# A transformer-like kernel of four layers: values turned through DRAM, and the relative terms added where the scores lie

## The chip, the cores and the metric

The kernel runs as one program on one core of a Trainium2 chip. A core has TensorE (PE, matrix products from SBUF into PSUM), VectorE (DVE), ScalarE (ACT), GpSimd (POOL) and SyncE (SP, which here only issues DMAs), each with a queue of its own; they wait for each other by semaphores. The metric is the device time of one execution in microseconds.

## What is computed

Four layers, each `x = x + layer(_gn(x))` on `x` of shape (4, 16, 16, 1024). Layer 0 is a lambda layer, layer 3 a tensor-train convolution; the change touches layers 1 and 2, which are attention over 16 heads of 64 channels. Layer 1 has a mask, layer 2 has position terms:

```python
# layer 1, per head
s = jnp.where(mask, jnp.einsum('bhqe,bhke->bhqk', q, k) * scale, min)
o = jnp.einsum('bhqk,bhke->bhqe', softmax(s), v)
# layer 2
qkv = hidden_states @ qkv_w + qkv_b
attn = jnp.einsum('bqc,bkc->bqk', q * scale, k)
rel_h = jnp.einsum('bhwc,hkc->bhwk', rq, Rh)
rel_w = jnp.einsum('bhwc,wkc->bhwk', rq, Rw)
attn = attn + rel_h[:, :, :, :, None] + rel_w[:, :, :, None, :]
out = softmax(attn, axis=-1) @ v
return out @ proj_w + proj_b
```

`rel_h` and `rel_w` use the query without the scale; `Rh` and `Rw` are rows of small tables, picked by the distance of key and query.

## The kernel before

Layers 1 and 2 are worked through in four stages `s` (layer 1 and 2, each in two halves of two images) of eight items `j`; an item `i = 8 s + j` is a pair of heads on 512 tokens. There are 32 items, 0 to 31 (`LAST`), of which 16 to 31 are layer 2. Every product is made of three float32r products (hi x hi, lo x hi, hi x lo), so a projection Q, K or V of one item is 8 chunks x 3 = 24 matmuls of 128x512, and one O block (output projection, eight per stage) as many.

The order of TensorE is written out in `attention_pe`: in an ordinary item scores(i) (`scores`, four banks from `S` = 2), `relative(i + 1)`, K(i + 1), `attend(i - 1)` (probabilities times values), V(i), and Q(i + 2) with `turn_values(i)` after its second chunk. In an item with j = 0 the eight O blocks of the stage before stand ahead of Q. In the last stage the first four chunks of O blocks 0, 1 and 2 are put between the last items' work, and `build_m` (a matrix for layer 3) between the rest.

The other engines, each in its own written order (`attention_act`, `attention_dve`):
- ScalarE evicts the products' high parts (`evac_q`, `evac_k`, `evac_v`, `evac_o`), takes the exponentials (`exps(i, k)`, four per item, one bank of 2 x 256 scores each), multiplies by the reciprocal sums (`normalize`), and evicts `relative`'s result (`evac_relative`). It also issues the write of the strips to DRAM.
- VectorE makes the low parts (`rest_of_q`, `rest_of_k`, `rest_of_o`), `maxima(i, k)`, the reciprocals (`invert_sums`), turns the probabilities in blocks of 32x32 (`turn_probs`), copies the values (`take_v`), adds O to `xT` (`add_out`) and makes the statistics (`stats_of`, `aggregate`, `group_stats`).
- In items with j = 1 to 4 both also make the next stage's norm: `norm.y` and `norm.head` on ScalarE, `norm.y` and `norm.rest` on VectorE; `norm.coefficients` (VectorE) comes before, after `norm.power` on GpSimd.
- The position terms: `relative(i)` multiplies the queries by the tables; the result goes to DRAM (`strips_to_dram`), and `strips_from_dram` reads it back with an offset per query, so that each query has its row term and its column term (`own_rel`). `sum_relative` adds both to a 512-wide tile `both_rel`, and `maxima` in layer 2 is one `scalar_tensor_tensor` (scores x SCALE + both_rel, in place) and one `tensor_reduce`.
- SP loads the weights in blocks of 256 KB (`w_load(n)`, three slots; GpSimd splits them into high and low part in `w_split`), and between them, at fixed places of the list of loads, the strips and the probabilities, which are written to DRAM and read back transposed (`probs_to_dram`, `probs_from_dram`, at `PROBS_AT`).

The values are turned on TensorE:

```python
for tt in range(4):
    m = nc.tensor.transpose(PS[:, turned_bank(i), tt * P:tt * P + P], vT[:, tt * P:tt * P + P], ident[:, :])
m.then_inc(v_tr, 1)
```

## Time and profile before

| | us |
|---|---|
| median of 3 runs (lowest, highest) | 1244.37 (1243.34, 1245.15) |
| the profiled execution | 1246.36 |
| its span | 1244.4 |
| TensorE busy | 1216.4 (98%) |
| VectorE, ScalarE, GpSimd busy | 690.4, 475.1, 641.5 |

The span is the time from the first to the last instruction. A matmul's busy time overlaps that of the next, so the distance between groups, not the busy time of one, is what a group costs. In the order of time, layer 0 takes 0 to 251 us, layer 1's two stages up to 706, layer 2's up to 1130 and layer 3 the rest.

### The profile page before, as it was taken

The numbers are of one execution on the slowest core, as the hardware profiler recorded it, in microseconds if no ns is written. First come the engines' busy times: TensorE is split into PE (matmuls) and PEld (weight loads), VectorE is DVE, ScalarE is ACT, GpSimd is POOL, SyncE is SP. The second block draws the span as 40 slices with busy tenths as digits, with TensorE's granted clock in tenths as the row PEclk, the third lists the DMA queues.
The fourth block names the chain that finished last, engine by engine and source line by source line (L and its number), as shares of the span: only waits on it lengthen the run. The fifth ranks groups of instructions, "written<-read, shape, count | busy, mean of one in ns | idle before, by whom it ended". The sixth has DMA issues, their size and how long they took to land.

```text
span 1244.4 us, 19555 instructions
## 1 busy us (share of the span) xinstructions
PE 1216.4 (98%) x6768; PEld 975.0 (78%) x6768; DVE 690.4 (55%) x1434; ACT 475.1 (38%) x1229; POOL 641.5 (52%) x726
## 2 busy tenths in 40 slices
PE   6999999999999999999999999999999999889998
PEld 4788896478888888888888878777887787668887
DVE  7534444775665433666452578756347776476212
ACT  3611141034645320656341164644206555243212
POOL 4633389256565567555546655555665556464000
PEclk9999999999999999999999999999999999999999
DMA  5211124025564643454645356557535565620012
GB/s 185 84 46 48 34 56 117 8 65 160 154 169 137 184 134 97 127 177 128 185 136 166 86 160 212 180 160 223 168 102 151 175 209 156 205 60 1 29 40 68
DMA packets 129376, 155.03 MB, mean 125 GB/s; under 512 B 30080, under 2 KB 84000, under 8 KB 129280
## 3 DMA queue, kind: packets, MB, share of 16 engines
q1 hardware_dynamic: 118976, 146.92, 39.7%
q10 hardware_dynamic: 10304, 6.88, 1.8%
q8 instruction: 54, 0.88, 0.3%
q14 instruction: 42, 0.34, 0.1%
HBM read 111.81 MB, written 37.75 MB: 120 GB/s over the span
## 4 chain that ended last, share of the span: by engine, by line
PE 89%; DVE 5%; ACT 2%; issue 1%; DMA 1%; SPq 1%; POOL 0%; ACTq 0%; DVEq 0%; POOLq 0%
PE PS L1137 53%; PE PS L682 7%; PE PS L1758 7%; PE PS L1183 4%; PE PS L960 3%; PE PS L969 2%; PE PS L975 2%; PE PS L1227 2%; PE PS L1216 2%; PE PS L1775 2%; PE PS L1247 2%; PE PS L665 1%; PE PS L1197 1%; DVE bst L257 1%; PE PS L700 1%
## 5 line engine op out<-in xcount | busy, mean ns | idle before, releaser
L1137 PE MATMUL PS<-XB,w_hi 128*128 128x512 f32 x1024 | 340.5, 397 | 1.2 <-POOL w_lo L228 1.2
L226 POOL CAST w_hi<-w_raw 128x512 fp32r<-128x512 f32 x195 | 124.2, 637 | 307.5 <-PE PS L1137 213.0
L228 POOL TENSOR_TENSOR w_lo<-w_raw,w_hi 128x512 fp32r<-128x512 f32 x195 | 256.1, 1313 | 15.6
L1137 PEld LDWEIGHTS PS<-XB,w_hi 128*128 128x128 f32 x1024 | 192.2, 188 | 47.1 <-issue 5.0
L1137 PE MATMUL PS<-XB,w_lo 128*128 128x512 f32 x512 | 200.2, 391 | 0.0
L1137 PE MATMUL PS<-XB,part 128*128 128x512 f32 x768 | 190.3, 394 | 0.0
L1137 PEld LDWEIGHTS PS<-XB,part 128*128 128x128 f32 x768 | 141.9, 188 | 32.2 <-issue 2.3
L1373 ACT ACTIVATE part<-PS,nmax 128x256 f32<-128x256 f32 (+1 forms) x256 | 112.2, 443 | 141.6 <-DVE nmax L1485 93.2
L1383 ACT ACTIVATE part<-part,prec 128x256 f32<-128x256 f32 (+1 forms) x256 | 105.8, 476 | 27.7 <-DVE prec L1500 27.7
L228 POOL TENSOR_TENSOR part<-part,part 128x512 fp32r<-128x512 f32 x85 | 111.5, 1312 | 6.8
L1137 PE MATMUL PS<-part,w_hi 128*128 128x512 f32 x344 | 112.9, 395 | 1.5 <-DVE part L1544 1.5
L226 POOL CAST part<-part 128x512 fp32r<-128x512 f32 x85 | 54.1, 636 | 116.3 <-PE PS L1137 103.7
L1137 PEld LDWEIGHTS PS<-XB,w_lo 128*128 128x128 f32 x512 | 96.2, 188 | 18.5 <-issue 0.2
L1496 DVE STREAM_TRANSPOSE part<-part 128x384 f32<-128x384 f32 (+1 forms) x128 | 82.1, 641 | 49.9 <-ACT part L1383 49.9
L1137 PEld LDWEIGHTS PS<-part,w_hi 128*128 128x128 f32 x344 | 65.2, 190 | 15.9 <-ACT part L1427 1.9
L682 PE MATMUL PS<-XB,w_hi 128*128 128x512 f32 x256 | 70.9, 392 | 0.0
L1137 PE MATMUL PS<-part,w_lo 128*128 128x512 f32 x172 | 67.6, 393 | 0.0
L1397 ACT ACTIVATE part<-PS,bias 128x512 fp32r<-128x512 f32 x16 | 11.0, 688 | 143.1 <-PE PS L1137 143.1
L1506 DVE COPY part<-PS 128x512 f32<-128x512 f32 x32 | 22.1, 692 | 78.2 <-PE PS L1197 78.2
L1137 PE MATMUL PS<-part,part 128*128 128x512 f32 x252 | 62.9, 399 | 0.2 <-issue 0.2
L1539 DVE TENSOR_TENSOR part<-part 128x512 f32<-128x512 f32 x64 | 59.4, 947 | 0.0
L598 DVE COPY part<-PS 64x512 f32<-64x512 f32 x32 | 34.6, 1080 | 44.2 <-PE PS L700 43.9
(136 smaller groups left out, 1884.0 us busy)
## 6 DMA issues: line engine op xcount, KB each, us to landing
w_raw<-in_w SPq DMA_DIRECT2D x187, 256.0 KB, 2.8
part<-in_w SPq DMA_DIRECT2D x85, 256.0 KB, 2.8
turned<-part SPq DMA_DIRECT2D x128, 128.0 KB, 2.9
part<-turned SPq DMA_DIRECT2D x32, 512.0 KB, 5.0
turned<-part SPq DMA_DIRECT2D x128, 96.0 KB, 2.5
part<-turned SPq DMA_DIRECT2D x32, 384.0 KB, 4.0
strips<-part ACTq DMA_DIRECT2D x16, 256.0 KB, 2.7
out_x<-xT SPq DMA_DIRECT2D x16, 256.0 KB, 2.1
```

Of the source, the lines that this page charges most:

```text
L226: pool.tensor_copy(hi, raw).then_inc(w_hi_done, 1)
L228: pool.tensor_tensor(lo, raw, hi.bitcast(F32), ALU.subtract).then_inc(w_ready, 1)
L598: last = nc.vector.tensor_copy(dst, src)
L682: m = nc.tensor.matmul(PS[:, 2 * (n % 2) + h, :], wt[:, (c % 4) * P:(c % 4) * P + P], x_part(hl, h, c), start=c == k == 0, stop=c == CK - ...
L960: m = nc.tensor.matmul(bank[0:rows * SIDE, (x - x0) * w:(x - x0) * w + w], table, Qs[:, jp, x * N + SIDE * y0:x * N + SIDE * y1], start=jp ...
L1137: m = nc.tensor.matmul(PS[:, bank, :], wt[:, (c % 4) * P:(c % 4) * P + P], rhs(hl, c), start=c == k == 0, stop=c == CK - 1 and k == 2)
L1183: m = nc.tensor.matmul(PS[:, S + 2 * a + hh, at + lo:at + hi], x[rows, qs], y[rows, cols], start=k == 0, stop=k == 2)
L1373: last = nc.scalar.activation(prob[:, n % 2, at:at + hi - lo], PS[:, S + k, qt * N + lo:qt * N + hi], ACT.Exp, bias=nmax[:, k, qt:qt + 1], ...
L1383: last = nc.scalar.activation(p, p, ACT.Copy, scale=prec[:, k, qt:qt + 1])
L1496: nc.vector.transpose(dst, src).then_inc(t_done, 1)
L1539: nc.vector.tensor_tensor(both_rel[:, n % 2, :, :, :], of_row, of_col, ALU.add).then_inc(rel_sum, 1)
L1758: m = nc.tensor.matmul(PS[:, bank, :], x3(hl, b, c, tt * P), w[:, c, half * HALF:half * HALF + HALF], start=c == k == 0, stop=c == CK - 1 ...
```

## The change

1. Values. `turn_values` moves from TensorE to VectorE: V's bank is turned in blocks of 32x32 into `vB`, written to DRAM in four pieces and read back (`values_to_dram`, `values_from_dram`), and `take_v`, now on ScalarE, copies it to `v`. `evac_v` is gone; V's bias is added to the attention's output in `evac_o` and `rest_of_o`.
2. `relative` has the tables as stationary and 512 queries as moving operand, three matmuls; its bank is turned by VectorE (`turn_relative`), and ScalarE issues four writes of strips, in runs of 32 elements, after the second `exps`.
3. `sum_relative` and `both_rel` are gone. `maxima` adds the row terms to the bank with one `tensor_tensor`, and then, for each half, adds the column terms, multiplies by -SCALE and takes the minimum in one `tensor_tensor_reduce`. The tables are divided by SCALE on GpSimd, and `exps` has a scale of -1 in layer 2.
4. Order. `attend(i - 1)` stands behind V(i) and Q(i + 2); with j = 0 Q(i + 2) stands ahead of the O blocks. `evac_o(i - 2)` and `rest_of_o(i - 2)` come in the middle of an item. Each item's probabilities go out in four writes instead of eight, a block of weights later. At the end the first halves of six O blocks, not three, stand between the last items.

TensorE in layer 2, from the last scores of item 25 to its K product, before (part_79 to part_82 are the queries, part_90 and part_91 the tables):

```order
L1183 MATMUL PS<-part_77,part_81 128x256 x2
L1247 MATMUL PS<-part_90,part_80 128x64 [waits v_evac_151,tables_ready_182,q_lo_155,q_hi_154]
L1247 MATMUL PS<-part_90,part_80 128x64
L1247 MATMUL PS<-part_91,part_80 128x64 x2
L1247 MATMUL PS<-part_90,part_82 128x64 x2
L1247 MATMUL PS<-part_90,part_80 128x64 x2
```

The same place now (part_88 and part_89 are the tables):

```order
L1177 MATMUL PS<-part_77,part_81 128x256 x2
L1225 MATMUL PS<-part_80,part_88 128x512 [waits tables_ready_180,q_lo_154,q_hi_153]
L1225 MATMUL PS<-part_80,part_89 128x512
L1225 MATMUL PS<-part_82,part_88 128x512
L1135 MATMUL PS<-XB,part_54 128x512 [waits w_ready_40,k_lo_156,k_hi_155]
```

Twelve rows with 24 matmuls have become three matmuls; the wait for `q_lo` has stayed in front of them.

ScalarE in a layer 2 item, from the second `exps` to the third, before (part_86 holds the probabilities, part_92 `all_rel`):

```order
L1373 ACTIVATE part_86,psum<-PS,nmax 128x256
L1383 ACTIVATE part_86<-part_86,prec 128x256 [waits p_rec_162,p_exp_161]
L1383 ACTIVATE part_86<-part_86,prec 128x256
L1383 ACTIVATE part_86<-part_86,prec 128x256 [waits p_rec_162,p_exp_161]
L1383 ACTIVATE part_86<-part_86,prec 128x256
L1407 ACTIVATE part_92<-PS 128x8x32 [waits rel_done_173,strips_out_175]
L1407 ACTIVATE part_92<-PS 128x8x32 [waits rel_done_173]
L1626 DMA strips<-part_92 128x4x128 [waits rel_evac_174]
L1373 ACTIVATE part_86,psum<-PS,nmax 128x256 [waits t_done_164,p_max_160]
```

And now (part_85 the probabilities, part_90 `all_rel`, part_83 `v`, part_84 `vB`, part_75 the attention's output):

```order
L1344 ACTIVATE part_85,psum<-PS,nmax 128x256
L1611 DMA strips<-part_90 512x1x32 [waits rel_evac_173]
L1611 DMA strips<-part_90 512x1x32 x3
L1354 ACTIVATE part_85<-part_85,prec 128x256 [waits p_rec_161,p_exp_160]
L1354 ACTIVATE part_85<-part_85,prec 128x256
L1354 ACTIVATE part_85<-part_85,prec 128x256 [waits p_rec_161,p_exp_160]
L1354 ACTIVATE part_85<-part_85,prec 128x256
L1333 ACTIVATE part_83<-part_84 128x512 [waits o_done_168,v_in_151]
L1390 ACTIVATE part_75<-PS,bias 128x512 [waits o_done_168]
L1344 ACTIVATE part_85,psum<-PS,nmax 128x256 [waits t_done_163,p_max_159]
```

The write of the strips stands ahead of both `normalize`, four issues instead of one; the values' copy and O's eviction have come before the third `exps`.

VectorE after the last O block of a stage, before:

```order
L337 TENSOR_SCALAR gn<-gn 128x1 [waits hn_step_63]
L342 COPY gn_wide<-gn 128x32 [waits hn_rstd_64]
L343 SCALAR_TENSOR_TENSOR gn_wide<-gn 128x32
L393 STREAM_TRANSPOSE coef<-gn_wide 128x64 [waits hn_wide_65]
L1515 SCALAR_TENSOR_TENSOR part_81<-PS,bias,part_79 128x512 [waits q_hi_154]
L1539 TENSOR_TENSOR part_83<-part_93 128x512 [waits rel_added_179,strips_in0_176] x2
L1482 SCALAR_TENSOR_TENSOR PS<-PS,part_83 128x512 [waits rel_sum_178,s_done_158]
L1485 TENSOR_REDUCE nmax<-PS 128x2 [waits rel_added_179]
```

And now (ISA is the `tensor_tensor_reduce`, and after each the read of its accumulator):

```order
L337 TENSOR_SCALAR gn<-gn 128x1 [waits hn_step_63]
L1457 TENSOR_TENSOR PS<-PS,part_91 128x512 [waits strips_in0_175,s_done_157]
L1462 ISA PS,nmax<-PS,part_91 128x256 [waits rel_added_177]
L1462 ISA nmax 128x1
L1462 ISA PS,nmax<-PS,part_91 128x256
L1462 ISA nmax 128x1
L1516 STREAM_TRANSPOSE part_90<-PS 128x512 [waits strips_out_174,rel_done_172]
```

The next item's first `maxima` follows the group statistics directly; the queries' low part has moved ahead of the O blocks' additions, and the coefficients to the end of the item.

The diff, without the semaphores' declarations and repeated details:

```diff
             take_block(i, "V", range(0 if i else 1, 2))
+            if i + 2 < ITEMS:
+                take_block(i + 2, "Q")
...
+    values = nc.dram_tensor("values", (2, P, 4 * P), F32).ap()
+    turned = nc.dram_tensor("turned", (2, P, 8 * N), F32).ap()
...
+            for k, (x, y) in enumerate(((rel_hi, qh[i % 2]), (rel_lo, qh[i % 2]), (rel_hi, ql[i % 2]))):
+                m = nc.tensor.matmul(PS[:, X, :], x.rearrange("p r n -> p (r n)"), y.rearrange("p (a y x) -> p y a x", a=2, y=SIDE),
+                                     start=k == 0, stop=k == 2)
+            m.then_inc(rel_done, 1)
...
         for i in range(1, LAST - 1):
             score_block(i)
             project(i + 1, "K", range(CK))
-            attend(i - 1, 0)
-            attend(i - 1, 1)
             project(i, "V", range(CK))
-            if i % PAIRS == 0:
-                s = i // PAIRS - 1
-                out_block(s, 0, range(CK))
-                out_block(s, 1, range(0, 2))
-                turn_values(i)
-                out_block(s, 1, range(2, CK))
-                for o in range(2, CK):
-                    out_block(s, o, range(CK))
+            if i % PAIRS:
                 project(i + 2, "Q", range(CK))
+                attend(i - 1, 0)
+                attend(i - 1, 1)
             else:
-                project(i + 2, "Q", range(0, 2))
-                turn_values(i)
-                project(i + 2, "Q", range(2, CK))
+                attend(i - 1, 0)
+                attend(i - 1, 1)
+                project(i + 2, "Q", range(CK))
+                for o in range(CK):
+                    out_block(i // PAIRS - 1, o, range(CK))
         i = LAST - 1
         score_block(i)
         project(LAST, "K", range(CK))
+        project(i, "V", range(CK))
         attend(i - 1, 0)
         attend(i - 1, 1)
-        project(i, "V", range(CK))
         scores(LAST, 0)
         scores(LAST, 1)
-        out_block(3, 0, range(0, 2))
-        turn_values(i)
-        out_block(3, 0, range(2, 4))
+        out_block(3, 0, range(0, 4))
         project(LAST, "V", range(CK))
+        for o in (1, 2):
+            out_block(3, o, range(0, 4))
         attend(i, 0)
         attend(i, 1)
-        out_block(3, 1, range(0, 4))
-        turn_values(LAST)
-        out_block(3, 2, range(0, 4))
-        for o in range(3):
-            out_block(3, o, range(4, 7))
+        for o in (3, 4, 5):
+            out_block(3, o, range(0, 4))
         attend(LAST, 0)
         attend(LAST, 1)
-        for o in range(3):
-            out_block(3, o, range(7, CK))
+        for o in range(6):
+            out_block(3, o, range(4, CK))
             for k in M_AFTER[o, 1]:
                 build_m(k)
-        for o in range(3, CK):
+        for o in range(6, CK):
             for half in range(2):
                 out_block(3, o, range(4 * half, 4 * half + 4))
                 for k in M_AFTER[o, half]:
                     build_m(k)
...
+        def take_v(i):
+            act.wait_ge(v_in, 16 * (i + 1))
...
+                act.wait_ge(o_done, 2 * i)
+            dst = v.rearrange("p t (b c) -> p t b c", b=4)
+            nc.scalar.activation(dst, vB.rearrange("p (b t c) -> p t b c", b=4, t=4), ACT.Copy).then_inc(v_ready, 1)
...
             j, s = i % PAIRS, i // PAIRS
-            if i:
+            if i and (i < PAIRS or j != 1):
                 evac_q(i + 1)
             exps(i, 0)
             exps(i, 1)
+            if LO_KEYS <= i + 1 < ITEMS:
+                strips_to_dram(act, i + 1)
             normalize(i, 0)
             normalize(i, 1)
-            evac_relative(i + 1)
+            if 0 < i < LAST:
+                take_v(i - 1)
+            if i >= 2 and j != 1:
+                evac_o(i - 2)
             exps(i, 2)
             normalize(i, 2)
+            if i == LAST:
+                take_v(i - 1)
             exps(i, 3)
-            if i and j == 0:
-                evac_o(i - 1)
             normalize(i, 3)
             evac_k(i + 1)
-            if j:
-                evac_o(i - 1)
-            evac_v(i)
             if 1 <= j <= 4:
                 for c in (2 * j - 2, 2 * j - 1):
                     norm.y(nc.scalar, s + 1, c)
                 for c in (2 * j - 2, 2 * j - 1):
                     norm.head(s + 1, c)
+            if i == LAST or i and j == 0:
+                evac_o(i - 1)
+            if i and j == 0:
+                evac_q(i + 2)
+        take_v(LAST)
...
-                dve.wait_ge(rel_sum, n - 4 * LO_KEYS + 1)
-                nc.vector.scalar_tensor_tensor(scores, scores, SCALE, both_rel[:, n % 2, :, :, :].rearrange("p a h w -> p (a h w)"),
-                                               ALU.mult, ALU.add).then_inc(rel_added, 1)
+                a, hh = k // 2, k % 2
+                dve.wait_ge(strips_in[a], 16 * 4 * (i - LO_KEYS + 1))
+                of_row, of_col = (own_rel[:, r, 2 * a:2 * a + 2, 32 * hh:32 * hh + SIDE] for r in range(2))
+                whole = scores.rearrange("p (a h w) -> p a h w", a=2, h=SIDE)
+                of_row = of_row.rearrange("p a (h w) -> p a h w", w=1).broadcast_to([P, 2, SIDE, SIDE])
+                nc.vector.tensor_tensor(whole, whole, of_row, ALU.add).then_inc(rel_added, 1)
                 dve.wait_ge(rel_added, n - 4 * LO_KEYS + 1)
-                last = nc.vector.tensor_reduce(nmax[:, k, :], scores.rearrange("p (a n) -> p a n", a=2), AX, ALU.max, negate=True)
+                for qt in range(2):
+                    tile = whole[:, qt, :, :]
+                    of_key = of_col[:, qt, :].rearrange("p (h w) -> p h w", h=1).broadcast_to([P, SIDE, SIDE])
+                    last = nc.vector.tensor_tensor_reduce(tile, tile, of_key, -SCALE, 3.0e38, ALU.add, ALU.min,
+                                                          accum_out=nmax[:, k, qt:qt + 1])
...
+        def turn_values(i):
+            product_done(dve, (i, "V"))
             if i:
-                dve.wait_ge(o_done, 2 * i)
-            nc.vector.tensor_copy(v.rearrange("p a n -> p (a n)"), PS[:, turned_bank(i), :]).then_inc(v_ready, 1)
+                dve.wait_ge(v_ready, i)
+            src = PS[:, bank_of(i, "V"), :].rearrange("p (t q c) -> p t q c", t=4, q=4)
+            dst = vB.rearrange("p (q t c) -> p t q c", q=4, t=4)
+            nc.vector.transpose(dst, src).then_inc(v_turned, 1)
...
+        def turn_relative(i):
+            if i == ITEMS or layer_of(i) == 1:
                 return
-            n, a, hh = 4 * i + k, k // 2, k % 2
-            dve.wait_ge(strips_in[a], 16 * 4 * (i - LO_KEYS + 1))
-            of_row, of_col = (own_rel[:, r, 2 * a:2 * a + 2, 32 * hh:32 * hh + SIDE] for r in range(2))
-            of_row = of_row.rearrange("p a (h w) -> p a h w", w=1).broadcast_to([P, 2, SIDE, SIDE])
-            of_col = of_col.rearrange("p a (h w) -> p a h w", h=1).broadcast_to([P, 2, SIDE, SIDE])
-            if n >= 4 * LO_KEYS + 2:
-                dve.wait_ge(rel_added, n - 4 * LO_KEYS - 1)
-            nc.vector.tensor_tensor(both_rel[:, n % 2, :, :, :], of_row, of_col, ALU.add).then_inc(rel_sum, 1)
+            dve.wait_ge(rel_done, i - LO_KEYS + 1)
+            if i > LO_KEYS:
+                dve.wait_ge(strips_out, 64 * (i - LO_KEYS))
+            nc.vector.transpose(all_rel, PS[:, X, :]).then_inc(rel_evac, 1)
...
-            if i:
+            if i and (i < PAIRS or j != 1):
                 rest_of_q(i + 1)
-            sum_relative(i, 0)
-            sum_relative(i, 1)
             maxima(i, 0)
+            turn_relative(i + 1)
             maxima(i, 1)
             invert_sums(i, 0)
-            sum_relative(i, 2)
             invert_sums(i, 1)
+            maxima(i, 2)
             turn_probs(i, 0)
-            maxima(i, 2)
             turn_probs(i, 1)
-            sum_relative(i, 3)
+            if i >= 2 and j != 1:
+                rest_of_o(i - 2)
+            maxima(i, 3)
             invert_sums(i, 2)
-            maxima(i, 3)
             turn_probs(i, 2)
-            if i and j == 0:
-                rest_of_o(i - 1)
+            if i == LAST:
+                turn_values(i)
             invert_sums(i, 3)
             turn_probs(i, 3)
             if i < LAST:
                 rest_of_k(i + 1)
-            if j:
+            if i < LAST:
+                turn_values(i)
+            if i and j == 0:
                 rest_of_o(i - 1)
-            if i and j == 0:
-                take_v(i)
-            if i and j == 0:
+                rest_of_q(i + 2)
                 for o in range(CK):
                     add_out(s - 1, o)
                     if o:
                 stats_of(s - 1, CK - 1)
                 norm.aggregate(s + 1, range(CK), 16)
                 norm.group_stats(s + 1)
-            if j or i == 0:
-                take_v(i)
-            if j == 0:
+            if j == 1:
                 norm.coefficients(s + 1)
...
+        sp.wait_ge(rel_evac, done + 1)
+        rows = strips[buf].rearrange("(ax y) n -> ax y n", y=SIDE)
+        for b in range(4):
+            src = all_rel[32 * b:32 * b + 32, :].rearrange("p (y n) -> p y n", y=SIDE)
+            sp.dma_start(rows[:, :, 32 * b:32 * b + 32], src).then_inc(strips_out, 16)
...
-    def probs_to_dram(sp, i, a):
+    def probs_to_dram(sp, i, a=None):
         run = 2 * squares(i) * 32
-        sp.wait_ge(t_done, 4 * i + 2 * a + 2)
+        sp.wait_ge(t_done, 4 * i + (2 if a == 0 else 4))
...
+            row = probB[32 * q:32 * q + 32, 0:8 * run].rearrange("p (b r) -> p b r", b=4)
+            at, w = (0, 2 * run) if a is None else (a * run, run)
+            to = bass.AP(turned.tensor, (i % 2) * P * 8 * N + 2 * q * run + at, [[8 * N, 32], [32 * 8 * N, 4], [1, w]])
+            sp.dma_start(to, row[:, :, at:at + w]).then_inc(p_out[a or 0], 16)
...
+    def values_to_dram(sp, i):
+        sp.wait_ge(v_turned, i + 1)
...
+        for b in range(4):
+            to = bass.AP(values.tensor, (i % 2) * P * 4 * P + P * b, [[4 * P, 32], [32 * 4 * P, 4], [1, P]])
+            sp.dma_start(to, vB[32 * b:32 * b + 32, :].rearrange("p (q r) -> p q r", q=4)).then_inc(v_out, 16)
+    def values_from_dram(sp, i):
+        sp.wait_ge(v_out, 64 * (i + 1))
+        sp.dma_start(vB, values[i % 2, :, :]).then_inc(v_in, 16)
...
+    STRIPS_AT = [slots[(i + 1, "K"), 1] if i < LAST else slots[(i, "V"), 0] for i in range(ITEMS)]
+    PROBS_AT = [slots[(i + 1, "V"), 1] for i in range(LAST - 1)] + [slots[(3, "O", 1), 0], slots[(3, "O", 5), 0]]
...
+                if n == PROBS_AT[i] and i < LAST:
+                    probs_to_dram(sp, i)
+                    values_to_dram(sp, i)
+                if n == PROBS_AT[i] + 1 and i < LAST:
                     probs_from_dram(sp, i, 0)
-                if n == PROBS_AT[i] + 2:
                     probs_from_dram(sp, i, 1)
+                if n == PROBS_AT[i] + 2 and i < LAST:
+                    values_from_dram(sp, i)
```

## Rows read from the trace of the kernel before

**Rows 1.** The page's part 1: busy us, share of the span, instructions of each engine.
```profile
PE 1216.4 (98%) x6768; PEld 975.0 (78%) x6768; DVE 690.4 (55%) x1434; ACT 475.1 (38%) x1229; POOL 641.5 (52%) x726
```

**Rows 2.** The chain in order of time, item 26: start us, us, what.
```profile
950.97 1.62 PE PS L1183 x24
952.59 1.51 PE PS L1247 x24
954.10 5.66 PE PS L1137 x24
959.77 1.88 PE PS L1216 x16
...
968.67 0.44 PE PS L1197 x4
...
973.24 1.62 PE PS L1183 x24
```

**Rows 3.** ScalarE's timeline in layer 1: start, us, instruction, idle before it.
```profile
344.00 0.60 ACT L1361 ACTIVATE part<-PS 128x512 f32<-128x512 f32 x1 [2.32 <-PE PS L1137]
```

**Rows 4.** TensorE's timeline: scores of item 30, layer 3's first product.
```profile
1040.01 1.69 PE L1183 MATMUL PS<-part,part 64*128 64x256 f32 x24
...
1129.94 8.34 PE L1758 MATMUL PS<-part,XB 128*128 128x512 f32 x36
```

**Rows 5.** TensorE's waits: us in total, times, longest us.
```profile
PE PS L1216 <- DMA part<-turned: 2.3, 4, 1.1
```

**Rows 6.** Issue of DMAs: SP's writes and reads of probabilities, ScalarE's queue in layer 0.
```profile
L1649 SPq DMA_DIRECT2D turned<-part x256: 303/442/1461, 284.9 to 1077.9; - x128
...
DMA to landing us min/median/max: 3.3/4.4/6.9
...
197.64 3.84 ACTq L900 DMA_DIRECT2D part<-part  x6
```

**Rows 7.** VectorE's timeline in item 18 (j = 2).
```profile
731.27 0.69 DVE L1482 SCALAR_TENSOR_TENSOR PS<-PS,part 128x512 f32<-128x512 f32 x1
...
732.60 0.69 DVE L1482 SCALAR_TENSOR_TENSOR PS<-PS,part 128x512 f32<-128x512 f32 x1
...
743.35 0.71 DVE L1496 STREAM_TRANSPOSE part<-part 128x512 f32<-128x512 f32 x1 [1.03 <-ACT part L1383]
...
746.87 0.73 DVE L408 TENSOR_SCALAR part<-xT,coef 128x256 f32<-128x256 f32 x2
748.04 2.56 DVE L419 TENSOR_TENSOR XB<-part,XB 128x512 fp32r<-128x512 f32 x2 [0.45 <-ACT XB L414]
```

**Rows 8.** ScalarE's timeline in the same item.
```profile
734.05 0.48 ACT L1373 ACTIVATE part<-PS,nmax 128x256 f32<-128x256 f32 x1 [0.31 <-DVE nmax L1485]
...
734.96 1.70 ACT L1383 ACTIVATE part<-part,prec 128x256 f32<-128x256 f32 x4
...
737.24 0.37 ACTq L1626 DMA_DIRECT2D strips<-part  x1
737.97 0.47 ACT L1373 ACTIVATE part<-PS,nmax 128x256 f32<-128x256 f32 x1 [0.76 <-DVE nmax L1485]
...
739.70 0.91 ACT L1383 ACTIVATE part<-part,prec 128x256 f32<-128x256 f32 x2 [0.72 <-DVE prec L1500]
741.10 0.47 ACT L1373 ACTIVATE part<-PS,nmax 128x256 f32<-128x256 f32 x1 [0.49 <-DVE nmax L1485]
```

**Rows 9.** VectorE's groups by line: busy us, mean ns, idle before.
```profile
L1539 DVE TENSOR_TENSOR part<-part 128x512 f32<-128x512 f32 x64 | 59.4, 947 | 0.0
...
L1475 DVE TENSOR_TENSOR PS<-PS,maskb 128x256 f32<-128x256 f32 x64 | 26.6, 415 | 1.2 <-PE PS L1183 1.2
```

**Rows 10.** VectorE's timeline after the last O block of stage 2.
```profile
923.28 0.75 DVE L1553 SCALAR_TENSOR_TENSOR xT<-PS,bias,xT 128x512 f32<-128x512 f32 x1 [4.03 <-PE PS L1137]
...
927.64 0.15 DVE L337 TENSOR_SCALAR gn<-gn 128x1 f32<-128x1 f32 x1
```

**Rows 11.** Busy us in one stretch of the tail, then granted clock, DMA share, GB/s.
```profile
1098.40:1101.40 3.00, 3.00 (x8) 2.32 (x7) 1.84 (x2) 0.19 (x1) 2.69 (x3) 0.50 0.02 8
```

208 lines of the change are left out of this document (88 added, 120 removed).

## The prediction

> **What bounds the kernel now.** I read four views. First the busy time: TensorE works in 1216.4 us of a span of 1244.4 us [rows 1], so almost all of the time is its own queue of matmuls, and an edit pays by what it takes out of that queue and costs by what it makes the queue wait for. Second the chain that ended last, in order of time. It shows one item of layer 2 with no gap: scores 1.62, `relative` 1.51, K, `attend` 1.88, V, the four transposes 0.44, Q, and the next scores 22.27 us after the last [rows 2]. Third, since TensorE is full, how near the others are to becoming the bound. In layer 1 ScalarE stands idle for 2.32 us before V's eviction [rows 3], with nothing queued behind it that TensorE needs. In layer 2, items with j = 1 to 4 also carry the norm of the next stage, and there VectorE and ScalarE have a chain of nearly the period's length (below). Fourth the end: from the scores of item 30 to layer 3's product the kernel takes 1129.94 - 1040.01 = 89.9 us, with several waits in it [rows 4].
>
> I call the start of the first `maxima` of an item m, counted from the start of the item's scores; it needs half of the 1.62 us of scores, so m is 0.85 where VectorE is free. A norm item is one with j = 1 to 4.
>
> **What leaves TensorE.** (a) `turn_values` goes: 32 times 0.44 us [rows 2] = 14.1 us. (b) `relative` becomes 3 matmuls of 512 columns instead of 24 of 64. The product's matmuls of the same width take 5.66 us for 24 [rows 2], so at most 0.24 each; without the change of tile shape they follow at 0.227, 24 in 5.46, or 0.68 for three. 1.51 - 0.68 = 0.83, 16 times = 13.3 us. The bounds are 0.68 and the 1.51 of before. (c) `attend` waited for its probabilities for 2.3 us in all [rows 5], at most 1.1 at a time; it now stands behind V and Q, 11 us later, which covers the way through DRAM. I count 0.7 us of it here and the rest in the tail.
> The period of a layer 2 item becomes 22.27 - 0.44 - 0.83 = 21.0 us.
>
> **The tail (d)**, by the new order, 0 at the scores of item 30: scores 1.62, relative 0.68, K 5.7, V 5.5, attend 1.9 end at 15.4. `scores(31)` then wait for `k_lo` until 18.3 (worked out below) and end at 20.0. Half an O block (2.75), V (5.5), two halves (5.5), attend (1.9) and three halves (8.2) end at 43.8. The second half of the last `attend` waits, in my count, until 45.5: the queue of SP has eight writes before it, 0.44 us each, and the read lands 4.4 us after its issue [rows 6]. The other 120 matmuls take 27.3, sixteen `build_m` 3.9, a wait on them 1.0, changes of shape 0.6. End at 79.4 instead of 89.9: 10.5 less, of which (a) and (b) hold 1.7. I take 8.5 us for the waits alone; between 4 and 10.
> Sum of what leaves: 14.1 + 13.3 + 0.7 + 8.5 = 36.6 us.
>
> **What the loop of VectorE and ScalarE costs.** In layer 2 the next `relative` needs `q_lo`, which VectorE makes after the norm's work. Before, from m (731.27) to the end of the norm's last subtraction (748.04 + 2.56 = 750.60) are 19.33 us [rows 7]. I change the path piece by piece:
> - From m to the second `exps`: 734.05 - 731.27 = 2.78 [rows 7, 8]. Now two maxima with `turn_relative` between them. A transpose of 512 columns is 0.71 [rows 7]. A maximum was two scans, 732.60 - 731.27 = 1.33 [rows 7]. Now it is one scan of 512 (0.69 and 0.04 for its semaphore) and two of 256, each with a read of its accumulator. The instruction isn't in the trace. A sum of 256 columns on a bank took 0.415 [rows 9], and I give the small read 0.1: 0.73 + 2 x 0.51 = 1.75. Bounds: 1.33, if the two are one scan; 2.3, if everything goes at the rate of the sum of two SBUF tiles, 0.947 for 512 [rows 9], with 0.2 per read. 2 x 1.75 + 0.70 + 0.05 = 4.25: +1.47.
> - Before the first `normalize` ScalarE now issues four writes of the strips. One took 0.37 [rows 8]; six others on this queue took 3.84, 0.64 each [rows 6]. I take 0.5: +2.0 (1.5 to 2.6). Behind them on ScalarE stand both `normalize`, and behind these VectorE's transposes.
> - From the end of both `normalize` (734.96 + 1.70) to the third `exps` 1.31 [rows 8], before for `evac_relative` and a wait; now `take_v` and `evac_o`, 0.65 each (a copy of 512 columns is 0.60 [rows 3]): 0.
> - Third `exps` to its `normalize` 1.73 [rows 8]; now `rest_of_o` 0.7, `maxima` 1.75 and the reciprocal with the hand-overs 0.3 stand before it, 2.75: +1.0. To the fourth `exps` 1.40 [rows 8], now 0.85, since its maximum is already there: -0.55.
> - From the last transpose of probabilities to the norm's `y` 3.52 (743.35 to 746.87 [rows 7]), which held `rest_of_o`, `take_v` and a wait for TensorE; now `rest_of_k` and `turn_values`, 1.95 in all: -1.57.
> - `rest_of_q` 0.7 closes the loop; the two sums of tables that followed it are gone.
> 19.33 + 1.47 + 2.0 + 1.0 - 0.55 - 1.57 + 0.7 = 22.4 us, against a period of 21.0. So each norm item is paced by this loop and TensorE waits 1.4 us at the next `relative`. `k_lo` comes at m + 17.4, early enough in the others, so items without a norm keep 21.0; in layer 1 no `relative` waits, and the loop is shorter.
> The first norm item (j = 1) costs more. Before, the Q product (5.5 us) lay between the last O block and the next scores, and covered VectorE's last sum, statistics and aggregate: 923.28 to 927.64 + 0.15, that is 4.5 us, about 4.6 from O's end [rows 10]. Now Q stands ahead of the O blocks, the cover is gone, and m = 4.6 instead of 0.85. The loop there is 22.3 (without `evac_o` and `rest_of_o` 1.35 less; `coefficients`, three small instructions like the one of 0.15 [rows 10] with their semaphores, 0.6 more, and ScalarE's `y` behind them 0.65). `q_lo` comes at 26.9, `relative` could start at 21.0 + 1.6 = 22.6: a wait of 4.3 us.
> A stage of layer 2 loses 4.3 + 3 x 1.4 = 8.5, two lose 17.0 us. With the low bounds of both prices the loop is 20.6 and 5 us are lost; with the high ones 24.6, and 34.6 us.
>
> **What I cost at nothing.** `turn_values` on VectorE in layer 1 and `take_v` on ScalarE take the place of `take_v` and `evac_v` there. The five DMAs of the values per item lie behind the probabilities' four (eight before) on SP; SP blocks on `v_turned` until about m + 18, but the next weights are needed some 6 us after that at the earliest. If that cover were gone TensorE would wait at a product for what SP is late.
>
> **A rule of the skill.** The strips were written in runs of 512 B and now in runs of 128 B (2048 a matrix). The landing of the write isn't critical in the trace: strips are issued by m + 7.2 and must be in DRAM by about m + 17. The Trainium skill, "DMA: Bandwidth & Descriptors", Specifications, says that below 512 B the DMA engine does read-modify-write, which speaks against this write; no run yet shows it here. A second, "Vector Engine (DVE) Microarchitecture Reference", section 7, says that the kind of instruction with an accumulator halves its rate with two SBUF sources that aren't bf16; here one is a PSUM bank, so by that page the 2.3 above wouldn't come and the maximum stays near 1.75.
>
> **The rivals.**
> 1. The loop fits: maximum 1.33, issues 0.37. Only the 2.5 us after each O stage stay: 36.6 - 5.0 = 31.6 off, 1212.8 us. For it: VectorE's pieces overlap in the trace. Against: four scans with reads where two stood.
> 2. Slower: the maximum with accumulator is slow. With x us above 1.75 the loop grows by 3x, a stage by 12x, both by 24x. The gain of 19.6 is gone at x = 0.8, a maximum of 2.55 us, or 0.9 us for each of the 256-column instructions with its read. At 3.0 it is 1244.4 - 19.6 + 30 = 1255. Nothing on a bank in the trace is so slow for its size.
> 3. The strips come late: if the small writes land after 11 us (2.7 before), the eight norm items wait 1 us more each: 1233.
> 4. It doesn't do what it says in part: `relative` reads its moving operand in runs of 16 and takes 1.5 us as before: 13.3 less, 1238.
> A fall of the clock could add to any: in the tail, after several waits, the granted clock was 0.50 for 3 us [rows 11] (the 1.2 GHz level), in which 8 matmuls ran instead of 13, 1.2 us lost. The waits of 4.3 us could bring two such stretches.
>
> **How the numbers follow.** The profiled execution has a span of 1244.4 and took 1246.36, 2.0 above the median of the runs; the gain is taken off the median. 36.6 - 17.0 = 19.6: 1244.4 - 19.6 = 1224.8, so 1225. Chances: this forecast 0.63, rival 1 0.14, rival 2 0.11, rival 3 0.06, rival 4 0.06. The range reaches from rival 1 with a slightly better tail, 1211, to 1241, which holds rivals 3 and 4 and most of the high bounds. A measurement of this kernel can tell about 0.2% from no change. Faster by more: the forecast, 1, 3 and 4 less their edges, 0.86; within 0.2% 0.04; slower 0.10.
>
> **What would show it.** Right: 0.44 us transposes and 64-column matmuls gone from the chain; items without a norm 21.0 us apart, in layer 1 20.0; waits of about 4 us at `relative` of items 18 and 26, about 1.4 in the three after each; `scores(31)` waiting about 3 us for `k_lo`. Wrong: the 256-column instruction far from 0.4 us, the ACT queue's issues far from 0.5, no wait at items 18 and 26, or waits at `attend` or at the products' weights.

## The result, and the profile after

The changed kernel takes **1264.57 us** (1262.71 to 1265.41, 4 runs) against 1244.22 us (1243.34 to 1245.15, 4 runs) for the kernel before on the same chip: a ratio of 1.016, 95% interval 1.0144 to 1.0179. The prediction was 1225 us, faster. It is slower by 20.3 us, 40 us off the forecast. The profiled execution has a span of 1263.0 us. The ratios, here and below, use the fast executions of each kernel alone.

In the kernel after, some names have other lines: `scores` L1177, `relative` L1225, `attend` L1198 (layer 2) and L1209 (layer 1); `take_v` on ScalarE L1333; `evac_o` L1390 and `rest_of_o` L1525; the maximum's two instructions L1457 (row term) and L1462 (column term, scale, maximum); `rest_of_k` L1505; on ScalarE's queue the strips' writes L1611; on SP's queue the probabilities' writes L1635 and reads L1646, the values' writes L1655 and read L1659, the strips' reads L1623.

The page's part 1 of after, for [rows 1]:
```profile
PE 1194.4 (95%) x6304; PEld 960.8 (76%) x6304; DVE 645.6 (51%) x1578; ACT 458.2 (36%) x1197; POOL 630.2 (50%) x727
```
TensorE is busy for 22 us less. The count was 27 us less; e5 below has the same matmuls, and they are busy for another 10 us less (1184.2), at a granted clock of 0.996 instead of 0.985. But it no longer works for nearly the whole span: 69 us of it are idle, against 28 before.

**Where the time went.** I took the starts of `scores` of all items from TensorE's timeline, which gives the period of each item. In layer 1 they are 19.7 us apart (before 20.4) as long as all is well, items 1 to 7 and 9 to 10. From item 11 on some take 20.2 to 21.9. In layer 2 they are 22.0, 27.1, 25.1, 23.0, 25.0, 21.8, 25.5 (items 17 to 23) and 21.5, 26.3, 24.1, 24.3, 24.8, 23.5 (25 to 30), where before nearly each took 22.3 (item 30: 17.0). Busy time in these two stretches, after first, then before (columns: from and to, us, busy time of PE, PEld, DVE, ACT, POOL, granted clock, DMA share, GB/s):
```profile
700.90:870.40 169.50, 153.65 (x808) 121.18 (x807) 100.97 (x275) 76.35 (x211) 80.21 (x85) 0.94 0.68 192
938.80:1083.30 144.50, 121.45 (x667) 96.34 (x667) 86.81 (x242) 65.80 (x182) 67.65 (x70) 0.98 0.67 188
```
```profile
705.70:862.80 157.10, 156.41 (x981) 124.01 (x980) 113.94 (x187) 81.81 (x226) 83.93 (x85) 1.00 0.58 174
928.60:1057.00 128.40, 127.87 (x815) 101.57 (x814) 96.89 (x162) 71.18 (x196) 71.54 (x70) 1.00 0.57 171
```
So the two stretches are 12.4 and 16.1 us longer. TensorE was busy for 2.8 and 6.4 us less in them, but stood idle for 15.9 and 23.1 us, and the granted clock, 1.00 before, was 0.94 and 0.98. Item 24, between them, takes 68.5 us instead of 65.8. Layer 1 (item 8 begins 6.3 us earlier, item 17 still 4.9) and the end (from `scores(31)` to layer 3's product 65.1 us instead of 73.0) give some of it back.

**What it waited for.** TensorE's waits of after, for [rows 5] (us in total, times, longest us):
```profile
PE PS L1225 <- issue: 17.0, 7, 2.9
PE PS L1177 <- DVE part L1505: 15.2, 11, 4.2
...
PE PS L1198 <- DVE part L1525: 6.1, 2, 3.8
```
`scores` wait for `k_lo`, `relative` for `q_lo` and `attend` for the `rest_of_o` of the item before. (The row of `relative` names no releaser; in item 18 `rest_of_q` ends at 727.33 and `relative` starts at 727.43.) All three come from VectorE, which is busy for only half of the time: it waits itself. ScalarE's waits show for what:
```profile
ACT part L1344 <- DVE nmax L1462: 161.1, 32, 49.4
ACT part L1333 <- DMA part<-values: 132.5, 31, 7.9
```
The second row is the one that matters. ScalarE stands for 132.5 us in front of `take_v`, in 31 of 32 items, since the values aren't back from DRAM. Item 22 shows how this reaches the others. ScalarE's timeline (start, us, instruction, idle before it):
```profile
829.23 1.39 ACTq L1611 DMA_DIRECT2D strips<-part  x2
830.73 1.71 ACT L1354 ACTIVATE part<-part,prec 128x256 f32<-128x256 f32 x4 [1.76 <-issue]
836.60 0.63 ACT L1333 ACTIVATE part<-part 128x512 f32<-128x512 f32 x1 [4.16 <-DMA part<-values]
837.14 0.67 ACT L1390 ACTIVATE part<-PS,bias 128x512 fp32r<-128x512 f32 x1
```
and the chain that ended last in the same stretch (start, us, what):
```profile
829.55 0.61 SPq L212
...
830.21 6.37 DMA part<-values
...
836.60 0.02 ACT part L1333
...
837.14 0.68 ACT part L1390
...
838.51 0.70 DVE PS L1457
...
843.91 0.72 DVE part L1505
...
844.88 1.70 PE PS L1177 x24
846.57 0.92 PE PS L1225 x3
847.49 2.75 PE PS L1135 x12
...
853.85 0.57 SPq L1646
...
855.13 6.95 DMA part<-values
```
This is a loop. The values' read of item 21 is issued at 830.21 and lands 6.37 us later. Behind it on ScalarE stand `take_v(21)`, `evac_o(20)` and the third `exps` of item 22, and so the second half of that item's softmax. Behind that on VectorE stands `rest_of_k(23)`, and `scores(23)` wait for it. Only when their product has used up weights can SP load new ones, and behind a load stand the probabilities' reads and the next values' read, 855.13. One turn takes 855.13 - 830.21 = 24.9 us; with TensorE never waiting it would be 21, by the prediction's count. The prediction called this place free.

Why does the read take so long? DMA issues of after, for [rows 6] (KB each, median us to landing):
```profile
values<-part SPq DMA_DIRECT2D x128, 64.0 KB, 2.5
part<-values SPq DMA_DIRECT2D x32, 256.0 KB, 5.9
```
A write of values lands after 2.5 us, the read of 256 KB after 5.9. On SP the read stands right behind two reads of probabilities (512 KB each in layer 2, 384 KB in layer 1) and a weight's load of 256 KB, so much of it may be time in a queue; e2 below tests that.

### The profile page after: what moved, and what is told of

Its sections match the earlier page's. It is cut to its first block, busy times and chain, and to the rows that moved or that the text cites. A ratio compares the mean times of both kernels' runs of the same rounds, so it can differ in the third digit from the quotient of the medians.

```text
span 1263.0 us, 18684 instructions
## 1 busy us (share of the span) xinstructions
PE 1194.4 (95%) x6304; PEld 960.8 (76%) x6304; DVE 645.6 (51%) x1578; ACT 458.2 (36%) x1197; POOL 630.2 (50%) x727
## 4 chain that ended last, share of the span: by engine, by line
PE 48%; DMA 13%; SPq 12%; DVE 10%; issue 7%; ACT 6%; POOL 3%; ACTq 1%; POOLq 0%; DVEq 0%
PE PS L1135 20%; DMA part<-values 11%; PE PS L1774 7%; PE PS L682 7%; SPq L1655 4%; SPq L1635 4%; PE PS L960 3%; SPq L212 2%; PE PS L969 2%; PE PS L975 2%; ACT part L1354 2%; DMA strips<-part 2%; PE PS L1791 2%; ACT part L1344 2%; SPq L1646 1%
## 5 line engine op out<-in xcount | busy, mean ns | idle before, releaser
L1135 PE MATMUL PS<-XB,w_hi 128*128 128x512 f32 x1024 | 335.4, 396 | 4.1 <-POOL w_lo L228 4.1
L226 POOL CAST w_hi<-w_raw 128x512 fp32r<-128x512 f32 x195 | 120.8, 619 | 327.1 <-PE PS L1135 172.7
L228 POOL TENSOR_TENSOR w_lo<-w_raw,w_hi 128x512 fp32r<-128x512 f32 x195 | 251.9, 1292 | 15.6
L1135 PEld LDWEIGHTS PS<-XB,w_hi 128*128 128x128 f32 x1024 | 194.9, 190 | 49.6 <-POOL w_lo L228 4.0
L1135 PE MATMUL PS<-XB,part 128*128 128x512 f32 x768 | 187.7, 393 | 0.0
L1135 PEld LDWEIGHTS PS<-XB,part 128*128 128x128 f32 x768 | 146.3, 191 | 31.2
L1135 PEld LDWEIGHTS PS<-XB,w_lo 128*128 128x128 f32 x512 | 97.4, 190 | 20.2 <-issue 0.2
L1135 PEld LDWEIGHTS PS<-part,w_hi 128*128 128x128 f32 x344 | 65.2, 190 | 15.5 <-issue 2.1
L1177 PE MATMUL PS<-part,part 64*128 64x256 f32 (+1 forms) x768 | 55.4, 292 | 19.4 <-DVE part L1505 15.2
L682 PE MATMUL PS<-XB,w_hi 128*128 128x512 f32 x256 | 70.9, 392 | 0.0
L1177 PEld LDWEIGHTS PS<-part,part 64*128 64x128 f32 x768 | 49.6, 194 | 27.8 <-issue 19.9
L1333 ACT ACTIVATE part<-part 128x512 f32<-128x512 f32 x32 | 20.2, 632 | 132.5 <-DMA part<-values 132.5
```

The lines of the kernel that those rows point to most:

```text
L226: pool.tensor_copy(hi, raw).then_inc(w_hi_done, 1)
L228: pool.tensor_tensor(lo, raw, hi.bitcast(F32), ALU.subtract).then_inc(w_ready, 1)
L682: m = nc.tensor.matmul(PS[:, 2 * (n % 2) + h, :], wt[:, (c % 4) * P:(c % 4) * P + P], x_part(hl, h, c), start=c == k == 0, stop=c == CK - ...
L1135: m = nc.tensor.matmul(PS[:, bank, :], wt[:, (c % 4) * P:(c % 4) * P + P], rhs(hl, c), start=c == k == 0, stop=c == CK - 1 and k == 2)
L1177: m = nc.tensor.matmul(PS[:, S + 2 * a + hh, at + lo:at + hi], x[rows, qs], y[rows, cols], start=k == 0, stop=k == 2)
```

## The experiments

**Theories.** T: the loop above, through `take_v`. R: the strips, written in runs of 128 B by four instructions instead of one in runs of 512 B, cost issue time on ScalarE and land late (median 5.8 us). M: the new maximum is slow. Each kernel was timed beside the one before on its chip. Items are numbered as above, and their lengths come from the starts of `scores` in the profiled execution.

### Take_v moved behind evac_k

```diff
-            if 0 < i < LAST:
-                take_v(i - 1)
             if i >= 2 and j != 1:
                 evac_o(i - 2)
...
             evac_k(i + 1)
+            if 0 < i < LAST:
+                take_v(i - 1)
```


> The changed kernel with one thing moved: ScalarE copies the values (take_v) behind evac_k instead of ahead of evac_o and the third exps. Theory T (the values' way through DRAM sets the pace: ScalarE stood 132.5 us before the 31 copies, with half of an item's softmax behind it): layer 2's items, 24 to 27 us apart now, come back to 21 to 23, and the kernel takes about 1245 us, 15 to 22 less than 1264.6. Rival R (the strips' small writes, landing after 5.8 us instead of 2.7, hold SP and all behind it): at most 4 us less. Rival M (the maximum's new form makes VectorE's loop too long): at most 4 us less.

Measured: 1230.66 us (1229.50 to 1231.78), ratio to before 0.989 [0.9873, 0.9902]. This is 34 us under the changed kernel, for an edit that removes no work and no DMA, and about twice what T expected: item 16 begins 8 us earlier than in the changed kernel, a gain in layer 1 that the expectation didn't count. `take_v`'s idle time, 132.5 us in the changed kernel, is here (us, times):
```profile
  DMA part<-values: 6.0, 4
```
The read still lands after 5.8 us, but nothing is behind it now. Items in layer 1 are 19.7 us apart throughout, in layer 2 mostly 20.2 to 22.4 (items 20, 26 and 28 take 26.2, 23.7 and 23.1).

### The values' read ahead of the probabilities' reads

```diff
                 if n == PROBS_AT[i] + 1 and i < LAST:
-                    probs_from_dram(sp, i, 0)
-                    probs_from_dram(sp, i, 1)
+                    values_from_dram(sp, i)
                 if n == PROBS_AT[i] + 2 and i < LAST:
-                    values_from_dram(sp, i)
+                    probs_from_dram(sp, i, 0)
+                    probs_from_dram(sp, i, 1)
```


> The changed kernel with the read of the values issued ahead of the two reads of the probabilities (1 MB) instead of behind them. T with the read's queueing as its cause: the values' read lands in about 3 us instead of 5.9 and starts about 1 us earlier, so each layer 2 item is up to 3 us shorter: about 1250 us. If the read's 5.9 us are not due to what is queued ahead of it: no change. Rivals R and M: no change.

Measured: 1228.03 us (1225.62 to 1233.87), ratio 0.988 [0.9844, 0.9908]. The second way to open the same loop gives the same, again more than the expectation had (1250 us). Issues, and `take_v`'s idle time:
```profile
part<-values SPq DMA_DIRECT2D x32, 256.0 KB, 3.1
```
```profile
  DMA part<-values: 35.4, 20
```
The read of the same 256 KB lands after 3.1 us in place of 5.9: 2.8 us were the queue. What is left on TensorE is the wait that the prediction spoke of, `relative` for `q_lo`:
```profile
PE PS L1225 <- issue: 13.3, 6, 3.2
```
It stands in items 18, 19, 21, 26, 27 and 29, which take 22.7 to 26.6 us, while nearly all others of layer 2 take 20.8.

### One write of the strips

```diff
-        for b in range(4):
-            src = all_rel[32 * b:32 * b + 32, :].rearrange("p (y n) -> p y n", y=SIDE)
-            sp.dma_start(rows[:, :, 32 * b:32 * b + 32], src).then_inc(strips_out, 16)
+        whole = strips[buf].rearrange("(t p) n -> p t n", p=P)
+        sp.dma_start(whole, all_rel.rearrange("p (t n) -> p t n", t=4)).then_inc(strips_out, 16)
```


> The changed kernel with the strips written by one DMA in runs of 512 bytes instead of four in runs of 128; the position terms are then those of wrong places, the work is otherwise the same. R: the whole loss of layer 2 goes, about 1240 us. T: ScalarE issues 1 DMA instead of 4 (some 2.3 us less an item) and SP gets its strips earlier, but the values still come last: 3 to 8 us less, about 1259. M: no change.

Measured: 1257.24 us (1253.87 to 1264.21), ratio 1.011 [1.0072, 1.0144]. This kernel leaves out the right places of the strips, so it computes wrong position terms with the same work. R is worth about 7 us here, the four executions reach from 0 to 11, and it doesn't explain the loss: ScalarE still waits for values, 167.9 us in all, and the loop stays closed.

### The kernel before, with the new maximum alone

Here `sum_relative` is gone and `maxima` is that of the change, with the tables scaled to fit it; the rest stays as it was.

> The kernel before with only the new form of the maximum (no sum_relative, tables divided by the scale on GpSimd, exps with a scale of -1). M: layer 2's items grow, 5 us or more slower than before. T and R: TensorE hides it, within 2 us of before; two sums of tables per item go and each maximum gets 0.2 us longer.

Measured: 1240.08 us (1239.72 to 1242.23), ratio 0.997 [0.9957, 0.9983]. M falls: this part alone is a gain of about 4 us (2 to 5 by the interval). In the trace of the changed kernel one whole maximum is (VectorE's timeline)
```profile
829.08 0.70 DVE L1457 TENSOR_TENSOR PS<-PS,part 128x512 f32<-128x512 f32 x1
829.81 0.43 DVE L1462 CUSTOM_DVE_ANT_1 PS<-PS,part 128x256 f32<-128x256 f32 x1
830.16 0.47 DVE L1462 CUSTOM_DVE_ANT_1 PS<-PS,part 128x256 f32<-128x256 f32 x1
```
829.08 to 830.63: 1.55 us, where I took 1.75, with bounds of 1.33 and 2.3. The first accumulator's read, 830.16 to 830.30, runs beside the second L1462.

### Both edits together

> The changed kernel with both earlier edits: take_v(i-1) behind evac_k(i+1) on ScalarE, and the values' read issued ahead of the probabilities' reads. Theory T (the take_v of one item, which waits for a read queued behind others, holds up the ScalarE work of the next item, in a loop): each edit alone opens that loop, so the two together give little over the better one: about 1225 us (1220 to 1228), items without a norm 20.8 us apart, the values' read landing after about 3 us. Theory L (what is left after that is the loop of VectorE and ScalarE in the norm items and at the stage boundary, as in the prediction): waits at relative in the norm items stay, 13 us or more in all. Rival Q (SP's queue is the second limit: values' and probabilities' transfers fill it whatever the order): 1230 or above, and waits at attend appear.

Measured: 1223.52 us (1221.45 to 1227.45), ratio 0.983 [0.9809, 0.9842]. With both ends of the loop open the changed kernel is 41 us faster and stands at the predicted time. ScalarE waits once more for values (7.1 us, the last item). What TensorE still waits for:
```profile
PE PS L1198 <- DMA part<-turned: 5.9, 5, 3.2
PE PS L1198 <- issue: 5.0, 4, 3.0
PE PS L1135 <- POOL w_lo L228: 3.8, 7, 1.2
PE PS L1209 <- issue: 3.8, 1, 3.8
PE PS L1225 <- issue: 3.0, 2, 1.5
```
The first and the third row are what SP brings, probabilities and weights. But most of the two rows of `attend` with no named releaser is `take_v`, now late on ScalarE. The 3.0 us are `attend(29)`; ScalarE's row and TensorE's:
```profile
1043.40 0.61 ACT L1333 ACTIVATE part<-part 128x512 f32<-128x512 f32 x1
1044.11 1.95 PE L1198 MATMUL PS<-part,part 128*64 128x256 f32 x16 [3.05 <-issue]
```
In item 16 it is the same: `take_v` ends at 643.71 and `attend(15)` starts at 643.81, after 3.79 us. So the late place has a price too.

### The Q product back behind the O blocks

The order of the stage boundary is as before the change, on TensorE and in the evacuations; all else as in the last kernel.

> e5 with the project(i + 2, 'Q') of a stage boundary back behind the O blocks, as it stood before. Theory L: the Q product covers VectorE's last sum, statistics and aggregate again; the prediction put 4.3 us of wait at relative of items 18 and 26 to this move, so the time falls by 5 to 9 us against e5 (of which 2 to 4 in the first norm item's scores). Rival S: the long first norm item is not from this cover, but from the strips' issues on ScalarE, so the time stays within 2 us of e5.

Measured: 1225.79 us (1223.24 to 1230.62), ratio 0.985 [0.9828, 0.9880]: no gain; L's 5 to 9 us didn't come. Items 18 and 26 now take 21.2 and 20.8 us instead of 22.5 and 22.5, and the ones after them 21.2 or less, so the cover that L speaks of is back. But items 8, 16 and 24, which hold the O blocks, take 65.7, 71.5 and 71.0 us against 63.5, 69.4 and 69.4: 2 us more each. TensorE's timeline shows a wait in each of them, 2.23, 2.22 and 1.61 us, at the O blocks, which now stand right behind `attend`; the releaser of the last is the `evac_o` on ScalarE. The gain at one end of the move is lost at the other.

### The strips issued behind normalize

```diff
-            if LO_KEYS <= i + 1 < ITEMS:
-                strips_to_dram(act, i + 1)
             normalize(i, 0)
             normalize(i, 1)
+            if LO_KEYS <= i + 1 < ITEMS:
+                strips_to_dram(act, i + 1)
```


> e5 with the four strips writes issued on ScalarE behind normalize(i, 1) instead of ahead of normalize(i, 0). Theory S (their issues, 0.56 to 2.0 us each by the profile of the change, delay normalize and so the VectorE work behind it): 2 to 3 us less in each of the six to eight norm items, 8 to 15 us off e5. Theory L without S (the loop is set by VectorE's own work): within 2 us of e5. Rival W (the strips' landing is late already): slower than e5, with waits of VectorE for strips at the next item's maxima.

Measured: 1223.33 us (1218.84 to 1227.77), ratio 0.983 [0.9802, 0.9857]. No difference from e5; the 8 to 15 us that S expected didn't come.

### One write of the strips, with the loop open

> e5 with the strips written by one DMA in runs of 512 B (in places that make wrong relative terms; the reads are as in the change). Theory S: like e7 or better, 8 to 15 us off e5, since three of four issues are gone and the write lands after about 2.7 us. Theory L without S: within 2 us of e5. If e8 gains and e7 does not, it is the landing and not the issue that costs.

Measured: 1213.04 us (1211.96 to 1214.76), ratio 0.975 [0.9733, 0.9763], 10.5 us under e5, in a kernel that leaves out the right places of the strips as e3 does. Its one write lands after 4.9 us (median), not after the 2.7 expected, and each of e5's four after 3.6. Ten of the twelve items 17 to 23 and 25 to 29 are now 20.8 us apart, all but two: item 18 with 25.3 and item 26 with 24.3. Item 18 on TensorE's timeline:
```profile
713.66 1.69 PE L1177 MATMUL PS<-part,part 64*128 64x256 f32 x24
718.24 0.96 PE L1225 MATMUL PS<-part,part 128*128 128x512 f32 x3 [2.90 <-issue]
```
and the windows of item 18 and of the one after it:
```profile
713.70:739.00 25.30, 22.41 (x119) 17.69 (x117) 19.69 (x41) 13.97 (x36) 13.66 (x14) 0.93 0.77 222
739.00:759.70 20.70, 20.70 (x117) 16.50 (x115) 15.65 (x37) 11.97 (x32) 11.35 (x13) 1.00 0.77 229
```
This is the wait at the boundary, in the item that the prediction named: 2.90 us idle, and a granted clock of 0.93 over the item, 0.50 (the 1.2 GHz level) from 719.2 to 722.0. Together it is about 4.5 us longer than its neighbour. In item 26 it is 1.90 us idle and 3.5 us in all.

### Take_v early at the boundaries, late elsewhere

```diff
-            if 0 < i < LAST:
+            if 0 < i < LAST and j == 0:
                 take_v(i - 1)
...
             evac_k(i + 1)
+            if 0 < i < LAST and j:
+                take_v(i - 1)
```
with the values' read first, as in e5.

> e5, but take_v(i-1) stands behind evac_k(i+1) only where j > 0; at a stage boundary (items 8, 16 and 24) it stands ahead of evac_o as in the change. Theory B: in e5 the late take_v costs at items 16 and 24, where attend(i-1) stands ahead of the O blocks and waits for it (69.4 us from item 16 and from item 24 to the next one, against 64.3 and 64.5 in e2): 5.1 + 4.9 = 10 us less than e5, so 1213 to 1215. Rival: those stages are long in e5 from the strips' issues or the DMA queue, so the time stays within 2 us of e5.

Measured: 1215.66 us (1212.81 to 1221.67, 5 runs), ratio 0.977 [0.9751, 0.9796]. 8 us under e5, and with the strips in their right places: **the best version, 29 us faster than the kernel before** (e13 below is level with it). The profiled execution is the slowest of the five, 1221.67 us. Item 16 takes 64.2 us (69.4 in e5), as expected. Item 24 didn't follow (69.6): there `attend(23)` waited 2.58 and 0.74 us for the probabilities' reads, which in this order stand behind the values'.

### The same narrow runs by one instruction

```diff
-        for b in range(4):
-            src = all_rel[32 * b:32 * b + 32, :].rearrange("p (y n) -> p y n", y=SIDE)
-            sp.dma_start(rows[:, :, 32 * b:32 * b + 32], src).then_inc(strips_out, 16)
+        to = bass.AP(strips.tensor, buf * HALF * P, [[32, 4], [SIDE * P, 32], [P, SIDE], [1, 32]])
+        sp.dma_start(to, all_rel.rearrange("p (y n) -> p y n", y=SIDE)).then_inc(strips_out, 16)
```


> e9 with the four strips writes of an item made by one instruction, to the same places in the same runs of 128 B. In e8 one instruction with runs of 512 B was 10 us better than e5. Theory I (it was ScalarE's time for issues, 4 x 0.66 us against 0.37): the gain comes here too as far as the instruction itself is short, so 3 to 9 us below e9. Theory D (it was the small runs in the DMA engines: they take the engines' time and delay the reads of the probabilities): within 2 us of e9, and the strips still land after 4 us or more.

Measured: 1286.04 us (1266.05 to 1290.45, 6 runs). The ratio, 1.023 [1.0178, 1.0279], uses the three shortest, 1266.05, 1280.95 and 1284.68 us (the profiled one): 50 to 69 us over e9, which neither theory expected. The issue is short, 0.53 us, but the chain shows when the write lands:
```profile
829.76 0.04 DVE part L1518
...
832.03 15.53 DMA strips<-part
847.58 0.63 SPq L1623
```
On this chain six such writes take 12.1 to 15.5 us; in e9 the median was 3.7. SP stands blocked in front of the strips' reads for that time, with the weights' loads behind it, and TensorE pays there:
```profile
PE PS L1135 <- POOL w_lo L228: 38.0, 12, 7.1
...
PE PS L1198 <- DMA part<-turned: 11.3, 2, 6.6
```
The Trainium skill, "DMA: Bandwidth & Descriptors", section "Why a DMA increments its semaphore by 16 and not by 1", has a rule that fits: one DMA is spread over the largest number of engines, up to 16, that divides the slowest dimension of both its access patterns. This destination begins with a dimension of 4 and its source with 128, so by this rule it would run on 4 engines, an estimate; the four separate writes begin with 32 on both sides, so on 16. The landing time agrees with it; which engines worked isn't shown by what I read. The run also shows what the prediction's third rival costs when it comes: not 1 us an item, but, through SP's queue, up to 11 (item 26 takes 33.1 us, in e9 22.4).

### Four writes of the strips in wide runs

> e5 (1223.5 us) with the strips still written by four instructions, but in runs of 512 B (in places that make wrong relative terms). e8, one instruction with runs of 512 B, was 1213.0. Theory I (ScalarE's time for four issues, 4 x 0.66 against 0.37 us, is what e8 saved): stays near e5 if an issue of wide runs takes as long as one of narrow runs, 1220 to 1225. Theory D (the 128 B runs cost DMA time and delay landings): near e8, 1211 to 1215. If an issue of wide runs is itself shorter, the times of the instructions in the profile tell how the two share.

Measured: 1215.25 us (1214.85 to 1216.28), ratio 0.976 [0.9742, 0.9769], near e8, as D had it (again without the right places of the strips). ScalarE's waits for its own issues ahead of `normalize`, in e5 and then here:
```profile
ACT part L1354 <- issue: 38.0, 16, 3.3
```
```profile
ACT part L1354 <- issue: 16.6, 10, 2.0
```
So of the 10.5 us about 2 are the number of instructions, and about 8 come with the width of the runs. But a narrow write is also issued more slowly (median 0.664 us against 0.467), so issue time and DMA time still change together.

### E9 with the strips behind normalize

> e9 (1215.7 us) with the four strips writes issued behind normalize(i, 1), as in e7. e7 was level with e5 (1223.3 against 1223.5). Theory I says that the issues cost on ScalarE wherever they stand in the item's first half: within 2 us of e9. If the place ahead of normalize is what costs, now that take_v no longer disturbs the stage boundaries, 3 us or more below e9.

Measured: 1220.27 us (1217.65 to 1225.02, 5 runs), ratio 0.980 [0.9782, 0.9826]. Not faster than e9, 4.6 us above it by the medians, with intervals that overlap; the place ahead of `normalize` isn't what costs.

### E9 with the strips issued by POOL

> e9 (1215.7 us) with the four strips writes issued from the queue of POOL instead of ScalarE's, behind the split of the fifth last weight before the strips are read; places and runs of 128 B as in the change. ScalarE has no issues left, the DMA engines have the same small packets. Theory I (ScalarE's issue time is what the narrow runs cost): ScalarE's 38 us of idle time on issues are gone and the time is that of one wide write on e9's base, 5 to 9 us below e9. Theory D (the small packets cost in the DMA engines): within 2 us of e9. Rival P: an issue holds up POOL, which makes the halves of the weights, and products wait for w_lo: slower than e9.

Measured: 1215.78 us (1212.45 to 1217.00, 5 runs), ratio 0.976 [0.9745, 0.9771], level with e9, which is what D expected. Yet the waits changed places. In e9:
```profile
PE PS L1135 <- POOL w_lo L228: 5.5, 8, 1.2
PE PS L1198 <- issue: 4.6, 3, 3.1
PE PS L1198 <- DMA part<-turned: 3.3, 2, 2.6
PE PS L1225 <- issue: 3.0, 2, 1.5
```
and with POOL's queue:
```profile
PE PS L1135 <- POOL w_lo L228: 10.4, 6, 6.2
PE PS L1135 <- POOL part L228: 2.9, 2, 1.6
```
The waits for `q_lo` are gone, those of `attend` but for 1 us, and TensorE waits for weights instead. One reading is that ScalarE's issue time did cost and that POOL now pays for it. POOL has 2.54 us of issues per item, and it also stands 22.4 us in all in front of them, waiting for `turn_relative`; the longest wait for weights, 6.16 us in item 30, comes behind 4.83 us of that. But it isn't shown: items 17 and 25 each wait 1.3 us for weights, and that alone gives VectorE time to have `q_lo` ready in items 18 and 26. How the 8 us of the narrow runs divide between issue time and the DMA engines stays open.

## Why the prediction was wrong, step by step

- **(a), (b), what leaves TensorE: right.** Without waits an item takes 19.7 us in layer 1 (predicted 20.0) and 20.8 in layer 2 (21.0). `relative` took 0.92 us in the chain with its change of shape, not 0.68. Layer 1 gains 0.7 us an item where (a) has 0.44; why isn't shown.
- **(d), the tail: within its bounds once the loop is open, but too favourable.** From `scores(30)` to layer 3's product the sum takes 1.7 + 8.5 us off 89.9, which leaves 79.7; e8 shows 82.0 and e5 83.5. So the waits gave back 6.2 and 4.7 us, not 8.5. In the changed kernel it was 1148.4 - 1059.8 = 88.6, since `scores(31)` waited 4.18 us for `k_lo` (about 3 predicted); in e5 and e8 they don't wait.
- **The maximum: 1.55 us measured, 1.75 taken.** Rival 2 is refuted, and e4 shows that the part is a gain.
- **The strips' issues: 0.66 us each, 0.5 taken**, 0.6 us more per item. The landing (5.8 us in the changed kernel, 3.6 in e5) was in time by the prediction's bound. Still e8 and e11 show 8 to 10 us in all for the width of the runs, which the sum didn't have. The Trainium skill, "DMA: Bandwidth & Descriptors", Specifications, has it that below 512 B the DMA engine does read-modify-write; it pointed the right way, but no run here shows that this is the reason.
- **The loop of VectorE and ScalarE: right in kind.** The waits at `relative` stand where the prediction put them. In the changed kernel they are 2.91 and 2.88 us in items 18 and 26, and 1.8 to 2.8 in five of the items after them (19, 21, 27, 28, 29), but there `take_v`'s wait is part of the path. With the loop open and four issues (e5) 1.49 and 1.48 us are left at the boundaries, behind waits at `attend` of 0.62 and 1.14 that already give VectorE time. With one issue (e8) they are 2.90 and 1.90 us; the prediction's own count with one issue of 0.37 and a maximum of 1.55 gives 4.3 - 2.0 + 0.37 - 0.6 = 2.1. That items 18 and 26 of e8 are 4.5 and 3.5 us longer, near the 4.3 of the sum, is luck: more than a third of it is the lower clock, which the sum left out. The 1.4 us in the other norm items can't be seen as waits at `relative` in e5, whose items 19 to 21 and 27 to 29 take 1.0 us more on average with their waits at `attend` and at the weights; with one wide write there is nothing (20.8).
- **The step that failed** is in the path from `normalize` to the third `exps`: "now `take_v` and `evac_o`, 0.65 each ...: 0", and with it "What I cost at nothing", where the values' DMAs were looked at only for what they hold up on SP. I counted how long `take_v` runs, and not when its input is there. It costs 132.5 us of ScalarE's time, and it closes a loop of 24.9 us in place of one of 21. Priced by e5 against the changed kernel it is 41 us, the size of the whole error. That e5 then lands at 1223.5, where 1225 was said, is in part luck. Against the kernel before, e5's profile gains 13.3 us up to the start of item 16 (8.6 by the sum), loses 0.8 from there to item 30 (0.8 gained by the sum) and gains 6.4 in the tail (10.2): three misses that nearly cancel.
- **The rivals.** None of the four is what happened. The slower side was on the list with a chance of 0.10, but with another mechanism. What the prediction named as signs of being wrong, "waits at `attend` or at the products' weights", is what e10 and e13 show. The change itself shows 6.1 and 3.3 us of waits at `attend` and 4.4 at the weights, but more at `scores` (19.3), which the list didn't have, and the reason, the values, wasn't on it.
- **The clock.** 1.00 in layer 2 before, 0.94 and 0.98 after. The prediction named such a fall as possible and left it out of the sum. In e8 it came behind the waits of 2.90 and 1.90 us at `relative` and cost 1.7 and 1.6 us on top. It doesn't follow every wait: in e5 the clock was 1.00 behind the waits of 1.49 (item 18) and 3.05 us (item 30).

## What to carry to other kernels

When an edit turns a result that was on chip into one that comes back through DRAM, the instruction that takes it up becomes a wait. Ask where it stands in the order of its engine, what is queued behind it, and when the transfer can have landed given all that stands ahead of it on its queue; then follow the path until it closes, across SP's queue and the weights too. Two edits that take no work away (take it up later, or read it first) were each worth 34 us and more here, and the profile names such a place in one row: an instruction of 0.6 us with 132.5 us of idle time before it. Where the late place is itself too late, the reader of the copy waits (3.79 and 3.05 us in e5), so the place is worth choosing by item, as in e9.

## What the runs showed of the hardware

- A read of 256 KB landed after 5.9 us (median, changed kernel) behind two reads of 384 or 512 KB and a weight's load on the same queue, and after 3.1 us (median, e2) ahead of those two reads.
- A write of the same bytes to the same places in runs of 128 B landed after 3.7 us (median, e9) as four instructions with 32 as the first dimension, and after 12.1 to 15.5 us (e10, six on the chain) as one instruction with 4 as the first.
- The issue of a 64 KB write in runs of 128 B took 0.66 us of ScalarE's time (median; up to 2.04, changed kernel) and 0.67 of POOL's (e13), 0.47 in runs of 512 B (e11), and a single one of 256 KB in runs of 512 B 0.37 (e8).
- The instruction that adds, scales and takes the extreme of 256 columns on a bank takes 0.45 us, the read of its accumulator 0.14, and of two such pairs the second starts 0.35 us after the first (changed kernel).
- TensorE's granted clock was 0.50 (the 1.2 GHz level) behind idle times of 2.90 and 1.90 us in e8, and 1.00 behind idle times of 1.49 and 3.05 us in e5.
